# Sandwich block on one core: whole-array transposes, one bank each, and a reordered list of blocks

## The chip, the core and the metric

The kernel runs on one core of a Trainium2 chip. The metric is device time in microseconds (us); the kernel before takes 1332.34 us, the median of three runs (1331.87 to 1333.54). The engines are TensorE (PE, its weight loads apart as PEld), VectorE (DVE), ScalarE (ACT), GpSimd (POOL) and the DMA queue of SyncE (SP).

## The reference

Eight batches of 1024 rows of 256 values, all float32. Attention with 16 heads of 16 values, then a channel mix; each is added to its input after a layer norm.

```python
q = x @ w_q.T; k = x @ w_k.T; v = x @ w_v.T            # x: layer norm of the input
scores = einsum('bqhd,bkhd->bhqk', q, k) * HEAD_DIM ** -0.5
concat = softmax(scores) @ v                            # per head, then heads side by side
x = x + _layernorm(concat @ w_o.T)
xn = _layernorm(x); x_prev = xn shifted by one row
xr = mu_r * xn + (1 - mu_r) * x_prev; xk = mu_k * xn + (1 - mu_k) * x_prev
out = sigmoid(xr @ W_r.T) * (square(relu(xk @ W_k.T)) @ W_v.T)
x = x + _layernorm(out)
```

## The kernel before

**The attention loop.** A unit `u` is half a batch (512 queries); `b = u // 2`, and 16 units follow each other. A unit has 32 steps: four quads of four heads (`qd`), each over eight blocks of 128 keys (`kt`). In step `i`, PE is given `scores(i + 1)` (L579: four matmuls, two heads at a time on the two halves of the array's rows, each into its half of a two-bank tile), then one piece of other work from `pump` (L302), then `values(i)` (L601: four heads side by side, 17 columns each, into one bank that is summed over eight steps). ACT does the two exponentials of a step (L596, 128x1024 each). `scores(i + 1)` overwrites the banks that the exponentials of step `i` read, so it waits for them.

**The other work** is written as lists of words, one list for even and one for odd units (EVEN, ODD, L845); unit 0 has FIRST before it. A word is a block: `T` turns four 128-row tiles of the normalized input into `xnT` (features on partitions), `Q`, `K` and `V`/`W` are projections of the next batch from `xnT`, and `y`, `z`, `k`, `r`, `v` are the output projection, the turn and the channel mix of the unit before. `T Q K V` form the chain "ahead", `y z k r v` the chain "behind"; within a chain the order is kept, and of two chains the word that stands earlier is asked first (`choose`, L219).

**Blocks and banks.** Three banks (`PM`) serve all this work. A matmul block (class Block, cost 2) needs one bank; it goes in two halves, the input rows 0 to 63 in two steps, the rows 64 to 127 in the next two, beside the first half of the block after it. A turn (class Turn, cost 2) needs two banks: in one step eight half-array transposes (64 rows to 64 columns) go to both banks at once, in the next step the other eight with banks exchanged (`begin`, L241). When its last matmul is given out, a block's `done` gives out the copies that empty its bank; a bank may be taken again `age` (1) steps after it was freed in the program's order, and PE then waits for the copy itself. Work after a `REST` goes on one step later, two such pieces a step.

**The pace.** `pump(left)` does one piece a step, and two where the cost of the waiting words exceeds the steps that are left in the unit (L307 to L311, only after step 9 and not in two steps running):

```python
need = sum(block.cost for block in waiting) + bool(tile[0] or tile[1]) + (turning[0] is not None)
doubled[0] = not doubled[0] and need > left and step_now[0] % 32 > 9
if doubled[0] or not left: step_part(age)
```

In unit 0 `left` is 0 up to step 9, so that these steps do two pieces.

**Queries and keys.** A finished Q or K block is split in two (L378, L444), stored by SP to a scratch tensor in device memory (L448) and read back spread over heads (`spread`, L501, reads at L508, all on SP's queue in the order in which they are given out). A store waits for the reads of the same scratch half. In unit 0 only quad 0 is projected directly; quads 1 to 3 come by `spread` at the steps in FIRST_SPREADS, quads 2 and 3 with both halves of queries and keys at once (steps 9 and 10), so that they need Q10, K10, Q11 and K11 stored. The weights `wq` and `wk` are split (L881, ACT and DVE) after the first scores are given out (L941).

**After the loop** the last unit's `y z k r v` run with nothing beside them (`run_all`).

Of the kernel before, what the change touches and what calls it, by code (L numbers as in the profile page):

```python
# [56 lines left out]
def sandwich_kernel(nc, x, wpack, consts, out):  # L57
    with ExitStack() as ctx:
# [59 lines left out]
        s_first = [[sem(f"s_first{i}"), 0] for i in range(4)]  # L118
# [66 lines left out]
        turning = [None]  # L185
# [3 lines left out]
        class Block:  # L189
# [3 lines left out]
            def __init__(self, chain, half, ready, done, queued=()):  # L193
                self.chain, self.half, self.ready, self.done = chain, half, ready, done
                self.seen, self.queued = None, queued

        class Turn:

            cost, banks = 2, 2

            def __init__(self, chain, halves, ready, done):
                self.chain, self.halves, self.ready, self.done = chain, halves, ready, done
                self.seen, self.queued = None, ()
# [37 lines left out]
        def begin(age):  # L241

            took[:] = 0.0, 0.0
            block = turning[0]
            if block is None:
                block = choose(age)
                if isinstance(block, Turn):
                    turning[0] = block
                    for a in range(2):
                        tile[a] = queue(block.halves[a](PM[block.bank[a]], a), *block.waits[a])  # L250
                    ends = [None, None]
                    emit(1e9, 1e9, ends)
                    block.ends = ends
                    return False
                now[:] = block, now[0]
                if now[0] is not None:
                    tile[0] = queue(now[0].half(PM[now[0].bank[0]], 0), *now[0].waits[0])
                if now[1] is not None:
                    tile[1] = queue(now[1].half(PM[now[1].bank[0]], 1), now[1].token)
                return bool(tile[0] or tile[1])  # L260
            for a in range(2):
                tile[a] = queue(block.halves[1 - a](PM[block.bank[1 - a]], a), block.ends[1 - a])
            ends = [None, None]
            emit(1e9, 1e9, ends)
            turning[0] = None
            until_rest(block.done(block.bank, ends[1]))
            return False
# [34 lines left out]
        def pump(left, age=1):  # L302
# [4 lines left out]
            need = sum(block.cost for block in waiting) + bool(tile[0] or tile[1]) + (turning[0] is not None)  # L307
# [5 lines left out]
        def run_all():  # L313

            while waiting or tile[0] or tile[1] or now[0] or turning[0] or resting:
# [21 lines left out]
        def token_half(name, still):  # L337
# [11 lines left out]
            return half  # L349

        def turn_half(src):

            def half(m, a):
                rows = rows_of(a)
                return [(.057, lambda e, t=t: e.transpose(m[:, t * 128 + 64 * a:t * 128 + 64 * a + 64],  # L355
                                                          src(t, rows), ident[rows, rows])) for t in range(4)]
            return half
# [49 lines left out]
        def p_turn(b, g):  # L407
# [4 lines left out]
            def done(banks, p):  # L412
                cols = slice(g * 512, g * 512 + 512)
                state["xA_read"] = p

                def split(c, k, m):
                    d = copy(xnT[0][:, c, cols], m[:, :], p, state["qk_read"])
                    d = dve.op(lambda e: e.tensor_tensor(xnT[1][:, c, cols], m[:, :], xnT[0][:, c, cols].bitcast(F32),  # L418
                                                         ALU.subtract), d)
                    free_bank(k, d)  # L420
                    xnt_ready[b, c, g] = d

                split(0, banks[0], PM[banks[0]])
                yield REST
                split(1, banks[1], PM[banks[1]])
            return Turn("ahead", [turn_half(lambda t, rows, c=c: xA[rows, 4 * g + t, c * 128:c * 128 + 128])
                                  for c in range(2)], ready, done)
# [8 lines left out]
        def p_qk(b, i, mt, n):  # L436
            cols = slice(n * 512, n * 512 + 512)

            def done(k, m, p):
# [6 lines left out]
                for j in range(2):  # L446
# [6 lines left out]
                         xnt_of(b, n, "wk"), done)  # L453

        def p_v(b, g):
# [4 lines left out]
            def done(k, m, p):  # L460
# [4 lines left out]
                v_ready[b, g] = d  # L465
                state["qk_read"] = p
            return Block("ahead", token_half("wv", still), xnt_of(b, g // 2, "wv"), done)
# [3 lines left out]
        def p_direct(i, p, n):  # L471
# [23 lines left out]
            return Block("ahead", half, xnt_of(0, n, "wide"), done)  # L495
# [206 lines left out]
        def o_z(u):  # L702

            def part(c, k, m, p):
# [8 lines left out]

            def done(banks, p):
                tk["A_read"] = p
                for c in range(2):
                    part(c, banks[c], PM[banks[c]], p)
                yield from mix(u)
            return Turn("behind", [turn_half(lambda t, rows, c=c: At[rows, t, c * 128:c * 128 + 128])
                                   for c in range(2)], have(("xn2", u, 0), ("xn2", u, 1)), done)  # L720
# [85 lines left out]
        def o_v(u, g):  # L806
# [29 lines left out]
            def still(i, c, t, rows):  # L836
# [71 lines left out]
        run("T0")  # L908
# [19 lines left out]
        def sum_all():  # L928
# [7 lines left out]
                       sum_all]  # L936
        run("D00 E00 D10 E10 T1 V0 V1 E01 E11")
# [3 lines left out]
        split_weights(["wq", "wk"])  # L941
        copier[0] = "dve"

        for u in range(2 * B):
# [6 lines left out]
            for s in range(32):  # L951
# [6 lines left out]
                pump(0 if u == 0 and s < 10 else 32 - s)  # L958
# [7 lines left out]
                if u == 0:  # L966
                    for work in FIRST_SPREADS.get(s, ()):
                        spread(0, *work)
# [12 lines left out]
        for word in "y0 y1 z k0 k1 r0 r1 v0 v1".split():  # L981
# [85 lines left out]
```

How the kernel before makes its waits and increments, by code:

```python
            def on_pe(e):  # L528
                for w_ in exps + all_here + [rows_all]:
                    e.wait_ge(w_[0], w_[1])
                for u in range(16):
                    a, p, qt = u // 8, u // 4 % 2, 4 * hf + u % 4
                    rows = slice(64 * a, 64 * a + SHIFT)
                    if u >= 2:
                        e.wait_ge(g_dve, 19 * n + u - 1)
                    for kh in range(2):
                        ins = e.matmul(PS[u % 2][:, kh, :], QS[qd][rows, p, qt * 128:qt * 128 + 128],
                                       KS[qd][rows, p, kh * 512:kh * 512 + 512], start=True, stop=True)
                    ins.then_inc(g_pe, 1)
                e.wait_ge(g_dve, 19 * n + 16)
                e.transpose(PS[0][0:16, 0, 0:128], mx[:, 0:16], ident[:, :]).then_inc(g_pe, 1)
                e.wait_ge(g_dve, 19 * n + 19)
                e.wait_ge(g_sp, 128 * (n + 1))
# [4 lines left out]
            def on_dve(e):  # L548
                for u in range(16):
                    e.wait_ge(g_pe, 17 * n + u + 1)
                    if u == 0 and n:
                        e.wait_ge(g_pe, 17 * n)
                    e.tensor_reduce(mx[:, u:u + 1], PS[u % 2][:, :, :], AX.XY, ALU.max).then_inc(g_dve, 1)
                e.wait_ge(g_pe, 17 * n + 17)
                if n:
                    e.wait_ge(g_sp, 128 * n)
                e.tensor_scalar(tmp[:, 0, :], PS[0][0:16, 0, 0:128], -1.0, None, ALU.mult).then_inc(g_dve, 1)
```

## Time and profile before

| | |
|---|---|
| median of the runs | 1332.34 us |
| the profiled execution's own time | 1331.7 us |
| its span, first to last instruction | 1329.9 us |
| PE busy, matmuls | 1261.8 us (95%), 10986 instructions |
| ACT busy | 1054.8 us (79%) |
| DVE busy | 788.3 us (59%) |
| exponentials, L596 | 1024 of 1024 ns |
| transposes, L355 | 512 half-array ones, in two groups of 256 |

The profile is one execution. Busy shares are means over stages with different limits, and a matmul's busy time overlaps that of its neighbours, so the time of a step is read from one start of the scores matmuls to the next. A row of the stretches view has the stretch in us from the span's start, its length, the busy time of each engine with its instructions, PE's granted clock (1.00 is 2.4 GHz, 0.50 is 1.2 GHz), the share of time in which the 16 DMA engines were busy, and GB/s.

### The profile page before, as it was taken

The numbers are of one execution on the slowest core, as the hardware profiler recorded it, in microseconds if no ns is written. First come the engines' busy times: TensorE is split into PE (matmuls) and PEld (weight loads), VectorE is DVE, ScalarE is ACT, GpSimd is POOL, SyncE is SP. The second block draws the span as 40 slices with busy tenths as digits, with TensorE's granted clock in tenths as the row PEclk, the third lists the DMA queues.
The fourth block names the chain that finished last, engine by engine and source line by source line (L and its number), as shares of the span: only waits on it lengthen the run. The fifth ranks groups of instructions, "written<-read, shape, count | busy, mean of one in ns | idle before, by whom it ended". The sixth has DMA issues, their size and how long they took to land.

```text
span 1329.9 us, 26219 instructions
## 1 busy us (share of the span) xinstructions
PE 1261.8 (95%) x10986; PEld 649.4 (49%) x10986; DVE 788.3 (59%) x1725; ACT 1054.8 (79%) x1153; POOL 271.7 (20%) x353
## 2 busy tenths in 40 slices
PE   7879999999999999999999999999999999999944
PEld 4533455455544555455544555455554555454433
DVE  5452574857466674757577484657657474545554
ACT  2568888888878888888888888888888888888821
POOL 1000122221221222212121222113221221222120
PEclk8899999999999999999999999999999999999967
DMA  4175194115633187124833166122932166101000
GB/s 146 56 172 164 35 179 93 43 60 116 135 66 95 49 146 116 43 65 101 139 81 96 49 129 126 35 80 74 166 81 64 31 114 135 42 2 33 1 17 16
DMA packets 60776, 112.75 MB, mean 85 GB/s; under 512 B 6256, under 2 KB 31088, under 8 KB 60592
## 3 DMA queue, kind: packets, MB, share of 16 engines
q1 hardware_dynamic: 60336, 109.60, 37.0%
q8 instruction: 104, 1.70, 0.6%
q10 hardware_dynamic: 288, 1.05, 0.2%
q14 instruction: 48, 0.39, 0.1%
HBM read 68.42 MB, written 41.94 MB: 83 GB/s over the span
## 4 chain that ended last, share of the span: by engine, by line
PE 80%; DVE 11%; ACT 4%; POOL 3%; DMA 2%; issue 1%; SPq 0%; POOLq 0%; ACTq 0%
PE O L608 31%; PE S L589 22%; PE M L345 13%; PE M L332 11%; ACT PT L596 3%; DVE sth L665 2%; DVE A L674 2%; POOL rsh L670 1%; PE M L355 1%; DVE T L628 1%; DVE A L812 1%; DVE mvh L667 1%; DMA KS<-scr 1%; DVE CC L632 1%; PE M L492 1%
## 5 line engine op out<-in xcount | busy, mean ns | idle before, releaser
L596 ACT ACTIVATE PT<-S 128x1024 f32<-128x1024 f32 x1024 | 991.4, 1024 | 191.3 <-PE S L589 190.5
L608 PE MATMUL O<-PT,V 128*17 128x512 f32 x4096 | 540.8, 600 | 0.2
L589 PEld LDWEIGHTS S<-QS,KS 50*128 50x128 f32 x2048 | 185.0, 184 | 469.4 <-ACT PT L596 424.9
L589 PE MATMUL S<-QS,KS 50*128 50x512 f32 x2048 | 390.4, 452 | 13.7 <-DMA KS<-scr 6.1
L669 POOL TENSOR_SCALAR veh<-mvh 128x2 f32<-128x2 f32 x96 | 22.1, 230 | 525.2 <-DVE mvh L667 525.2
L332 PE MATMUL M<-xnT,WH 64*128 64x512 f32 x512 | 115.1, 402 | 3.3 <-DVE xnT L418 1.9
L608 PEld LDWEIGHTS O<-PT,V 128*17 128x17 f32 x4096 | 67.9, 95 | 101.6 <-issue 54.0
L812 DVE SCALAR_TENSOR_TENSOR A<-Z,M 128x512 f32<-128x512 f32 x30 | 20.4, 682 | 158.5 <-PE M L345 158.5
L345 PE MATMUL M<-WH,cT 64*128 64x256 f32 x512 | 87.5, 288 | 9.4 <-DVE cT L642 5.4
L345 PE MATMUL M<-WH,B 64*128 64x256 f32 x512 | 84.7, 281 | 3.6 <-DVE B L746 3.6
L345 PE MATMUL M<-WH,xnT 64*128 64x256 f32 x512 | 86.7, 283 | 1.4 <-DVE xnT L418 1.4
L378 DVE CAST p<-M 128x512 fp32r<-128x512 f32 x62 | 42.3, 683 | 72.2 <-PE M L332 50.9
L345 PE MATMUL M<-WH,C 64*128 64x256 f32 x512 | 83.2, 278 | 1.1 <-DVE C L776 1.1
L332 PEld LDWEIGHTS M<-xnT,WH 64*128 64x128 f32 x512 | 67.4, 189 | 14.8 <-DVE xnT L418 4.5
L345 PEld LDWEIGHTS M<-WH,cT 64*128 64x128 f32 x512 | 68.3, 193 | 12.8 <-issue 6.3
L735 POOL TENSOR_TENSOR C<-A,C 128x512 fp32r<-128x512 f32 x30 | 38.6, 1287 | 162.9 <-DVE C L378 162.9
L332 PE MATMUL M<-xnT,WL 64*128 64x512 f32 x256 | 71.5, 397 | 0.0
L332 PE MATMUL M<-C,WH 64*128 64x512 f32 x256 | 64.0, 410 | 7.6 <-DVE C L735 6.9
L670 POOL TENSOR_TENSOR rsh<-veh,half 128x2 f32<-128x2 f32 x96 | 69.0, 719 | 8.0
L345 PEld LDWEIGHTS M<-WH,xnT 64*128 64x128 f32 x512 | 67.6, 188 | 1.9 <-DVE xnT L418 1.6
L345 PEld LDWEIGHTS M<-WH,B 64*128 64x128 f32 x512 | 66.3, 187 | 4.4 <-DVE B L746 4.2
L764 POOL TENSOR_TENSOR scratch<-scratch 128x512 f32<-128x512 f32 x30 | 32.9, 1096 | 164.0 <-DVE scratch L762 164.0
(112 smaller groups left out, 1617.9 us busy)
## 6 DMA issues: line engine op xcount, KB each, us to landing
scr<-p SPq DMA_DIRECT2D x124, 256.0 KB
QS<-scr SPq DMA_DIRECT2D x60, 256.0 KB, 6.4
KS<-scr SPq DMA_DIRECT2D x60, 256.0 KB, 11.1
QS<-scr SPq DMA_DIRECT2D x66, 128.0 KB, 7.0
xA<-x_dram SPq DMA_DIRECT2D x16, 512.0 KB, 6.9
KS<-scr SPq DMA_DIRECT2D x64, 128.0 KB, 10.2
xB<-x_dram SPq DMA_DIRECT2D x16, 512.0 KB, 6.6
out_dram<-xB SPq DMA_DIRECT2D x15, 512.0 KB, 3.1
```

The costliest lines, as they stand in the source:

```text
L332: out.append((.216, lambda e, k=k, w=w, v=moving(j, c, rows): e.matmul(m[:, :], w, v, start=(a == 0 and k == 0), stop=(a == 1 and k == 5))))
L345: out.append((.117, lambda e, k=k, t=t, w=w, v=still(i, c, t, rows): e.matmul(m[:, t * 256:t * 256 + 256], v, w, start=(a == 0 and k == 0) ...
L378: return dve.op(lambda e: e.tensor_copy(dst, src), *waits)
L589: fn = lambda e, p=p, a=a, rows=rows: e.matmul(PS[p][:, a, :], KS[qd][rows, p, kt * 128:kt * 128 + 128], QS[qd][rows, p, hf * 512:hf * 512 ...
L596: e_fn = lambda e, p=p: e.activation(PT[i % 2][:, 2 * p:2 * p + 2, :], PS[p][:, :, :], ACT.Exp, scale=SCALE)
L608: fn = lambda e, j=j: e.matmul(PO[32 * j:32 * j + 17, :], V[b % 2][:, kt, 4 * qd + j, :], PT[i % 2][:, j, :], start=(kt == 0), stop=(kt == 7))
L665: toks = [dve.op(lambda e, t=t: e.bn_stats(sth[:, 2 * g + t, :], src(t)), *ready) for t in range(2)]
L670: r = pool.op(lambda e: e.tensor_tensor(rsh[:, ts], veh[:, ts], half[:, 0:2], ALU.pow), p)
L674: return dve.op(lambda e: e.tensor_scalar(dst, src, mvh[:, n, 0:1], rsh[:, n:n + 1], ALU.subtract, ALU.mult), *waits)
L735: tk["xk", u, c] = side().op(lambda e: e.tensor_tensor(C[1][:, cols], A[:, cols], C[0][:, cols].bitcast(F32), ALU.subtract), d)
L764: tk["sq", mt] = k1, r, side().op(lambda e: e.tensor_tensor(r[:, :], r[:, :], r[:, :], ALU.mult), d)
L812: d = dve.op(lambda e: e.scalar_tensor_tensor(out=A[:, cols], in0=sig_of(u, g), scalar=1.0, in1=m[:, :], op0=ALU.add, op1=ALU.mult), p, tk ...
```

## The change

A turn becomes four transposes of whole 128x128 tiles into one bank, in one step (cost 1, one bank), so each `T` and each `z` becomes two words, one for each half of the features. A turn isn't taken while the block that still has its second half to do reads the same rows of `xnT`. The lists are set anew; the key and query reads of quads 2 and 3 in unit 0 go by halves and from steps 7, 8 and 10, each with a semaphore of its own; `wq` and `wk` are split once V0 is done in the prelude; unit 0 stops doing two pieces a step one step earlier; and in steps 8 to 19 of the last two units a block is taken two steps, instead of one, after its inputs and its bank were given out. `turn_half` goes, and `p_turn`, `o_z` call `done` for one bank.

```diff
         class Turn:
-            cost, banks = 2, 2
+            cost, banks = 1, 1
...
+                    if isinstance(block, Turn) and now[0] is not None and now[0].tokens == block.tokens is not None:
+                        return None
                     waiting.remove(block)
...
+            block = choose(age)
+            if isinstance(block, Turn):
+                k, = block.bank
+                for t in range(4):
+                    fn = lambda e, t=t: e.transpose(PM[k][:, t * 128:t * 128 + 128], block.src(t), ident[:, :])
+                    if t < 3:
+                        pe.quiet(fn, *(block.waits[0] if t == 0 else ()))
+                    else:
+                        p = pe.op(fn)
+                until_rest(block.done(k, PM[k], p))
+                return False
...
-            need = sum(block.cost for block in waiting) + bool(tile[0] or tile[1]) + (turning[0] is not None)
+            need = sum(block.cost for block in waiting) + bool(tile[0] or tile[1])
...
         def p_v(b, g):
...
                 v_ready[b, g] = d
+                if meanwhile:
+                    meanwhile.pop(0)()
...
-        FIRST = "Q00 K00 V2 K01 V3 Q10 K10 Q11 K11 Q01"
-        EVEN = "W3 T0 y0 y1 T1 z k0 k1 r0 r1 v0 v1 Q00 K00 Q01 K01"
-        ODD = "y0 y1 z k0 k1 r0 r1 v0 v1 Q10 K10 Q11 K11 V0 V1 V2"
+        FIRST = "Q00 K00 V2 K01 V3 Q10 K10 K11 Q01 Q11"
+        EVEN = "W3 T00 T01 y0 y1 Q00 T10 T11 z0 z1 k0 k1 r0 r1 v0 v1 K00 Q01 K01"
+        ODD = "y0 y1 z0 z1 k0 k1 r0 r1 v0 v1 Q10 K10 Q11 K11 V0 V1 V2"
...
-        FIRST_SPREADS = {3: [(1, (0, 1), (0,), s_first[0])], 6: [(1, (1,), (1,), s_first[1])], 9: [(2,)], 10: [(3,)],
-                         16: [(0, (0,), (1,), s_first[2]), (1, (0,), (1,), s_first[3])]}
+        FIRST_SPREADS = {3: [(1, (0, 1), (0,))], 6: [(1, (1,), (1,))], 7: [(2, (0, 1), (0,))], 8: [(2, (1,), (1,))],
+                         10: [(3, (0, 1), (0,)), (3, (1,), (1,))], 16: [(qd, (0,), (1,)) for qd in range(4)]}
...
-        run("T0")
+        run("T00 T01")
...
         meanwhile[:] = [lambda: ln1_norm(0, 1), lambda: (split_weights(["wv"]), sum_heads()),
-                       sum_all]
-        run("D00 E00 D10 E10 T1 V0 V1 E01 E11")
+                       sum_all, lambda: None, lambda: split_weights(["wq", "wk"])]
+        run("D00 E00 D10 E10 T10 T11 V0 V1 E01 E11")
...
         scores(0)
-        split_weights(["wq", "wk"])
...
-                pump(0 if u == 0 and s < 10 else 32 - s)
+                age = 2 if b + 1 == B and 8 <= s < 20 else 1
+                pump(0 if u == 0 and s < 9 else 32 - s, age)
...
-        for word in "y0 y1 z k0 k1 r0 r1 v0 v1".split():
+        for word in "y0 y1 z0 z1 k0 k1 r0 r1 v0 v1".split():
```

## Rows read from the trace of the kernel before

**Rows 1.** The page: its first line, and the line of busy times.

```profile
span 1329.9 us, 26219 instructions
...
PE 1261.8 (95%) x10986; PEld 649.4 (49%) x10986; DVE 788.3 (59%) x1725; ACT 1054.8 (79%) x1153; POOL 271.7 (20%) x353
```

**Rows 2.** Stretches view, units 0, 2, 3, 14 and 15, from scores to scores.

```profile
41.42:135.28 93.86, 84.53 (x609) 38.69 (x609) 40.28 (x81) 64.67 (x70) 3.81 (x5) 0.91 0.56 140
...
210.38:287.45 77.07, 75.83 (x676) 37.55 (x672) 47.57 (x98) 64.69 (x71) 16.05 (x20) 1.00 0.32 76
287.45:362.37 74.92, 74.84 (x692) 39.63 (x688) 49.37 (x116) 64.74 (x71) 18.61 (x24) 1.00 0.53 107
1122.61:1197.12 74.51, 72.38 (x608) 34.92 (x604) 39.60 (x89) 64.40 (x71) 18.23 (x23) 1.00 0.17 37
1197.12:1268.75 71.63, 69.73 (x568) 31.51 (x564) 37.10 (x84) 62.34 (x69) 16.17 (x22) 1.00 0.05 16
```

**Rows 3.** Stretches view, PE alone: steps 1, 2-3, 4, 10-12 of unit 2; 29-30 of unit 0.

```profile
212.73:215.12 2.39, 2.39 (x28) 1.00 0.99 156
215.12:219.31 4.19, 4.05 (x44) 1.00 1.04 137
219.31:222.60 3.29, 2.63 (x28) 1.00 0.94 194
234.44:243.18 8.74, 8.33 (x70) 1.00 0.00 1
129.22:133.17 3.95, 3.75 (x28) 1.00 0.47 140
```

**Rows 4.** Timeline of PE, unit 2, steps 2 to 4: start, length, line.

```profile
215.12 0.74 PE L589 MATMUL S<-QS,KS 50*128 50x512 f32 x4
215.68 0.42 PE L355 MATMUL M<-ident,xA 64*128 64x64 f32 x8
216.03 1.05 PE L608 MATMUL O<-PT,V 128*17 128x512 f32 x8
217.02 1.13 PE L589 MATMUL S<-QS,KS 50*128 50x512 f32 x4
...
220.72 0.35 PE L345 MATMUL M<-WH,cT 64*128 64x256 f32 x1 [0.66 <-POOL xB L823]
```

**Rows 5.** Groups by line, whole-array 128x128 products of the prelude: count, busy us, mean ns.

```profile
L897 PE MATMUL S<-A 128*128 128x128 f32 x16 | 2.1, 281 | 1.6 <-DMA A<-w_dram 1.6
L897 PEld LDWEIGHTS S<-A 128*128 128x128 f32 x16 | 1.9, 191 | 2.4 <-DMA A<-w_dram 2.4
```

**Rows 6.** Timeline of DVE, unit 2: the second splits after turns.

```profile
219.88 0.69 DVE L418 TENSOR_TENSOR xnT<-M,xnT 128x512 fp32r<-128x512 f32 x1
...
237.19 0.69 DVE L418 TENSOR_TENSOR xnT<-M,xnT 128x512 fp32r<-128x512 f32 x1
```

**Rows 7.** Stretches view, PE alone: unit 0, steps 0-1, 2-9 and 14-16.

```profile
41.42:53.71 12.29, 10.53 (x42) 0.58 0.00 1
53.71:78.14 24.43, 24.43 (x221) 1.00 0.51 151
87.84:102.28 14.44, 8.35 (x59) 0.76 1.04 159
```

**Rows 8.** Timeline of PE, unit 0: the waits in step 0 and at step 15.

```profile
44.18 1.22 PE L332 MATMUL M<-xnT,WH 64*128 64x512 f32 x2 [1.35 <-DVE WL L881]
...
95.89 1.22 PE L589 MATMUL S<-QS,KS 50*128 50x512 f32 x4 [6.09 <-DMA KS<-scr]
```

**Rows 9.** DMA view, 50 to 135 us, key reads: count, KB each, median us to landing.

```profile
KS<-scr SPq DMA_DIRECT2D x8, 128.0 KB, 4.6
...
KS<-scr SPq DMA_DIRECT2D x4, 256.0 KB, 10.7
```

**Rows 10.** Stretches view, PE alone: unit 14, step 18.

```profile
1163.07:1166.53 3.46, 2.81 (x19) 1.00 0.02 5
```

**Rows 11.** Timeline of PE after the loop: the first block waits.

```profile
1274.11 0.55 PE L345 MATMUL M<-WH,cT 64*128 64x256 f32 x1 [5.36 <-DVE cT L642]
```

More of the change, by code:

```diff
@@ L117, in sandwich_kernel @@
         s_qk = [[sem(f"s_qk{i}"), 0] for i in range(4)]
-        s_first = [[sem(f"s_first{i}"), 0] for i in range(4)]
+        s_first = [[sem(f"s_first{i}"), 0] for i in range(10)]
         s_rows, s_wide = [sem("s_rows"), 0], [sem("s_wide"), 0]
@@ L191, in sandwich_kernel, with __init__ @@
             cost, banks = 2, 1
-            def __init__(self, chain, half, ready, done, queued=()):
+            def __init__(self, chain, half, ready, done, queued=(), tokens=None):
                 self.chain, self.half, self.ready, self.done = chain, half, ready, done
-                self.seen, self.queued = None, queued
+                self.seen, self.queued, self.tokens = None, queued, tokens
         class Turn:
-            cost, banks = 2, 2
-            def __init__(self, chain, halves, ready, done):
-                self.chain, self.halves, self.ready, self.done = chain, halves, ready, done
-                self.seen, self.queued = None, ()
+            cost, banks = 1, 1
+            def __init__(self, chain, src, ready, done, tokens=None):
+                self.chain, self.src, self.ready, self.done = chain, src, ready, done
+                self.seen, self.queued, self.tokens = None, (), tokens
         def until_rest(work):
@@ L243, in begin @@
             took[:] = 0.0, 0.0
[L244 to L267, printed above, removed]
+            block = choose(age)
[9 more added lines that the diff above has]
+                return False
+            now[:] = block, now[0]
+            if now[0] is not None:
+                tile[0] = queue(now[0].half(PM[now[0].bank[0]], 0), *now[0].waits[0])
+            if now[1] is not None:
+                tile[1] = queue(now[1].half(PM[now[1].bank[0]], 1), now[1].token)
+            return bool(tile[0] or tile[1])
         def emit(limit0, limit1, ends):
@@ L313, in run_all @@
         def run_all():
-            while waiting or tile[0] or tile[1] or now[0] or turning[0] or resting:
+            while waiting or tile[0] or tile[1] or now[0] or resting:
                 pump(0, 0)
@@ L348, in half @@
                 return out
[L349 to L356, printed above, removed]
             return half
@@ L405, in ln1_norm, with p_turn, done @@
             state["ln1"][b, g] = d
-        def p_turn(b, g):
+        def p_turn(b, g, c):
             def ready():
                 return (state["ln1"][b, g], c_here) if (b, g) in state["ln1"] else None
-            def done(banks, p):
+            def done(k, m, p):
                 cols = slice(g * 512, g * 512 + 512)
                 state["xA_read"] = p
[L416 to L427, printed above, removed]
+                d = copy(xnT[0][:, c, cols], m[:, :], p, state["qk_read"])
+                d = dve.op(lambda e: e.tensor_tensor(xnT[1][:, c, cols], m[:, :], xnT[0][:, c, cols].bitcast(F32),
+                                                     ALU.subtract), d)
+                free_bank(k, d)
+                xnt_ready[b, c, g] = d
+            return Turn("ahead", lambda t: xA[:, 4 * g + t, c * 128:c * 128 + 128], ready, done, g)
         def xnt_of(b, g, *more):
@@ L465, in done @@
                 v_ready[b, g] = d
+                if meanwhile:
+                    meanwhile.pop(0)()
                 state["qk_read"] = p
-            return Block("ahead", token_half("wv", still), xnt_of(b, g // 2, "wv"), done)
+            return Block("ahead", token_half("wv", still), xnt_of(b, g // 2, "wv"), done, tokens=g // 2)
         def p_direct(i, p, n):
@@ L494, in half @@
                 return out
-            return Block("ahead", half, xnt_of(0, n, "wide"), done)
+            return Block("ahead", half, xnt_of(0, n, "wide"), done, tokens=n)
         meanwhile = []
@@ L700, in o_y, with o_z, done @@
             return Block("behind", token_half("wo", still), have(("cT", u, 0), ("cT", u, 1), more=("wr",)), done)
[L702 to L704 removed]
+        def o_z(u, c):
+            def done(k, m, p):
                 d = copy(Z[:, c, 1:513], m[:, :], p, tk.get("Z_read"), *(part_read[2] if u == 0 else ()))
@@ L712, in part @@
                 tk["z", c] = [d, d0]
[L714 to L720, printed above, removed]
+                if c:
+                    tk["A_read"] = p
+                    yield from mix(u)
+            return Turn("behind", lambda t: At[:, t, c * 128:c * 128 + 128], have(("xn2", u, 0), ("xn2", u, 1)), done)
         def mix(u):
@@ L967, in sandwich_kernel @@
                     for work in FIRST_SPREADS.get(s, ()):
-                        spread(0, *work)
+                        spread(0, *work, s_first.pop())
                 if u == 0 and s in (2, 3, 4, 5):
```

3 lines of the change are left out of this document (1 added, 2 removed).

## The prediction

> **What bounds the kernel.** I read the page first. PE is busy for 95% of the span, ACT for 79% [rows 1]. That is a mean, so I cut the loop into units with the stretches view, from the start of one step's scores to another's. There the reader sees three kinds of unit: unit 0 takes 93.86 us, even units such as unit 2 take 77.07, odd units such as unit 3 take 74.92 [rows 2] (units 4, 6, 8, 10 and 12 repeat the one, 1 to 13 the other). Then single steps. A step with half a block in it takes about 2.36 us, scores, half block and values end to end on PE: (74.92 - 4.19) / 30 if the two transposing steps of an odd unit cost what those of unit 2 cost [rows 2, 3]. The step of 2.39 in [rows 3] is one of these. A step with nothing in it takes 3.95 / 2 = 1.98 [rows 3]: there ACT's exponentials set the pace. So PE sets a step that has work, ACT one that has none, and a unit's time is the sum over its steps plus what PE waits for. 32 steps at 2.36 make 75.5; unit 0 and the even units lie above what their work needs.
>
> **Where the even unit loses.** Steps 2 and 3 hold the two phases of T0 and take 4.19. Step 4 takes 3.29: PE starts its half block 1.41 after the scores (219.31 to 220.72) where 0.56 is usual (215.12 to 215.68) [rows 3, 4]. The row names POOL's add, but y0 doesn't read that; the bank it takes is one that T0 gave back, and DVE's split of it ends at 219.88 + 0.69 = 220.57 [rows 6]. Steps 10 to 12 take 8.74 [rows 3]: T1 waits two steps for a second bank, both its phases fall in a doubled step 10, Q00 then waits for `xnT`, and step 12 is doubled, since the words still waiting cost more than the steps left. z takes steps 14 and 15, 4.2 as in T0. Together 4.19 + 3.29 + 8.74 + 4.2 = 20.42 for eight steps.
>
> **A turn's price, step by step.** Before, eight half-array transposes stand between scores and values for 0.35 (215.68 to 216.03); scores take 0.56 before them, values 0.99 to the next scores (216.03 to 217.02) [rows 4]. Afterwards four 128x128 transposes stand there. The trace has no such transpose; the nearest row is the prelude's whole-array float32 product, 16 records in 2.1 us with a mean of 0.281, so (2.1 - 0.28) / 15 = 0.12 from start to start, its weight loads of 0.191 hidden beside them [rows 5]. I take 4 x 0.12 + 0.1 to drain = 0.58, and a step of 0.56 + 0.58 + 0.99 = 2.13, against 4.19 / 2 = 2.10 before. From below, 0.35 as before, and ACT's 1.98 is the floor. From above, 0.24 a transpose, since the eight products of L897 show as 16 records and a transpose might need two as well: 1.06, a step of 2.61. I take 0.12 because today's transposes show one record each (512 for 512). So a turn is no faster on PE: what may be gained is that it needs one bank and no second phase.
>
> The Trainium skill, in "TensorE: Matmul & The Clock Gate", section "Part 4: PE-mode transpose", speaks against this price: about 275 ns for one 128x128 transpose inside a kernel. If that were the spacing, the four would take 4 x 0.275 + 0.1 = 1.2 and the step 2.75, and the sum below would come out as about 1342. Today's eight in 0.42 us [rows 4] don't bear that out as a spacing.
>
> **The even unit after.** I walked the new list through the rule for choosing. Steps 0-1 W3; 2 T00; 3 T01; 4-5 y0; 6-7 y1; 8-9 Q00; 10 T10; 11 T11; 12-13 K00; 14 z0; 15 z1; 16-19 Q01, K01; 20-31 k, r, v. The need never exceeds the steps left (22 of 22 at step 10, 20 of 20 at step 12), so nothing is doubled, and step 8, where the second half of y1 had gone alone, carries Q00. T00's split is given to DVE one step earlier, ahead of v1's norm, so the bank that y0 takes is free in time: the 0.85 wait goes. Next late is DVE at step 11. It is full in that stretch, T11 takes the bank that T10 has just left, and the matching split ended at 237.19 + 0.69 = 237.88, 3.44 after step 10's scores at 234.44 [rows 3, 6]; T11 wants it at 2.13 + 0.56 = 2.69, so it waits 0.75 and the values behind it on PE, and then ACT, wait along. Sum of the same eight steps: T00, T01, T10, z0, z1 5 x 2.13, T11 2.13 + 0.75, y0 and K00 2 x 2.36 = 18.25. Saved: 2.2 a unit, six units (2 to 12): **-13**. Odd units keep their order; two turns at +0.03: **+0.4** over seven.
>
> **Unit 0.** Step 0: PE waits 1.35 for the split of `wk` [rows 8], and the copies for it stand between ACT's exponentials. Steps 0 and 1 take 12.29 at a mean clock of 0.58 [rows 7], that is mostly at 1.2 GHz, after a stretch in which PE had little to do. With the weights split in the prelude, beside V1, the wait and the two ACT copies (about 1.2) go: 1.5 off for certain. If PE, busy sooner, keeps 2.4 GHz, the two steps take about 3.7 + 3.05 = 6.75, that is 5.5 off. The rows don't tell which; I take **-3.5** and keep both ends. Steps 2 to 9 hold two pieces and take 24.43 / 8 = 3.05 [rows 7]; step 9 now has one: -0.7, and step 10 carries half a block in place of a doubled turn: **-1** together. The large term is the wait for keys: steps 14 to 16 take 14.44, 6.09 of it a wait for the key read of quad 2, and PE comes back at half clock (0.76 on average) [rows 7, 8]. Before, the whole read was given out in step 9 (at 78.14 - 3.05 = 75.1) and the keys landed 20.8 later. Now the first halves go out in step 7, without Q11 and K11 before them (one 3.05 step less), and as half reads, 4.6 to land (a group that mixes quad 1's half reads with parts of whole ones) and not 10.7 [rows 9]: about 20.8 - 3.05 - 6.1 = 11.7 after step 7 begins. They are wanted at step 15, 2 x 3.05 + 6 x 2.3 = 19.9 after it. A margin of 8, so the wait goes and steps 13 to 16 (16.8) become two half blocks and two turns, 9.4 with 0.4 for DVE: **-7.4**. What could be late next on SP's queue, the second half of these keys (a store that waits for the first read, then 4.6) and quad 3's, is wanted four and eight steps later. The 16 reads at step 16 hold up batch 1's stores, and DVE may stand for some 10 us on a store, as it does today; nothing on PE needs it before unit 1. The last half block ends one step earlier: **-0.4**. Prelude: the copy of a turn's first half need not wait for its second phase, T00/T01 and T10/T11: **-1** (0 to -1.5).
>
> **The last two units.** With age 2, z starts a step later and k0 two steps later in unit 14; the wait in step 18 (3.46 against 2.36 [rows 10]) and that before z go, -2.5. But two steps of v1 move into unit 15, its y0 waits 0.9 longer for `cT`, and its own v1 ends after the loop. There y0 stands 5.36 behind the last quad's DVE work [rows 11], and now about four more DVE operations of 0.7 [rows 6] come before it: up to +2.8, I take +2.2. With z0's copy starting earlier at the end: **0** together (-2.5 to +3).
>
> **Sum** against the profiled execution's 1331.7 (span 1329.9): -13 + 0.4 - 3.5 - 1 - 7.4 - 0.4 - 1 + 0 = -25.9, so 1305.8. That run stands 0.6 below the median of 1332.34; I say **1306**. Its own range: -2 to +2 for the clock of steps 0-1, -9 if a turn is only as long as ACT's step (58 turns in the loop x 0.15), +5 for a turn dearer by 0.08, 3 each way for the last units: 1296 to 1314.
>
> **Rivals.** (1) *The first unit keeps its wait.* The scratch goes through one SP queue with stores that wait for reads, and DMA engines are full there (share 1.04) [rows 7]; if the first halves come no sooner and PE falls to 1.2 GHz again, -7.4 and 2 of the 3.5 are lost: 1315. Against it: less than half as much is read at once. Chance 0.16. (2) *The even units slip a step.* The plan fits exactly, so one late bank means a doubled step, and T11's wait takes the place of y0's; at worst 77.07 stays: 1319. Chance 0.1. (3) *Whole-array transposes don't hide their weight loads.* Each then shows its load and its matmul, 0.191 + 0.12 [rows 5]: 4 x 0.31 + 0.1 = 1.34, 0.76 more in each of 58 turn steps, all on PE: +44, **1350**, slower. It decides from 25.9 / 58 = 0.45 a turn on, or 0.23 from one transpose to the next; two records each (0.24) would give about 1334. For it: today two row halves load beside each other, which ends. Against it: [rows 5] hide the load on the whole array. Chance 0.07.
>
> **Chances.** Forecast 0.67, rivals 0.16, 0.1 and 0.07. Leaving out (3) and the edges, 1296 to 1320 holds 8 in 10. A measurement of this kernel can tell 0.2%, 2.7 us. Faster 0.92, same 0.02, slower 0.06.
>
> **What would show it.** In the profile after: 8 x 16 x 2 = 256 transposes of 128x128; turn steps near 2.13 with a start-to-start of 0.12; no wait before y0; about 0.75 of waiting in step 11 behind DVE's split; even units near 74.9; no DMA wait of PE in unit 0, which takes about 81.5, and clock 1.00 from its step 2 on; y0 after the loop later by about 2. I am wrong if transposes are 0.2 or more apart, if even units stay above 76, or if PE still waits for `KS<-scr`.

## The result and the profile after

The changed kernel takes 1315.38 us, the median of four runs (1312.64 to 1317.79), beside 1332.11 (1331.22 to 1333.54) for the kernel before on the same chip: a ratio of 0.9873, 95% interval 0.9851 to 0.9894. It is faster by 1.3%. The forecast of 1306 was 9 us too low. The wide range (1296 to 1320) holds the result; the forecast's own (1296 to 1314) misses it by 1.4, and the number lies on the 1315 of rival 1, so it takes the profile to say which mechanism it was. The profiled execution took 1315.18, so it can be set against the one before: 16.5 us less.

First the page, span and busy times, to be read against [rows 1]:

```profile
span 1313.4 us, 25725 instructions
...
PE 1260.9 (96%) x10730; PEld 645.5 (49%) x10730; DVE 783.2 (60%) x1726; ACT 1056.3 (80%) x1153; POOL 271.0 (21%) x352
```

256 matmul records fewer (512 half-array transposes became 256), yet PE's busy time is the same. So nearly all of the gain is time in which PE had stood still. The stretches view, units 0, 2, 3 and 14 from scores to scores, and unit 15 to the end of the last exponential (columns as in [rows 2], whose last row ends 1.1 later, with the last values):

```profile
39.47:122.43 82.96, 81.95 (x593) 37.70 (x594) 37.72 (x77) 63.41 (x68) 3.82 (x5) 0.96 0.53 145
...
198.07:273.55 75.48, 75.03 (x652) 36.82 (x648) 46.67 (x98) 64.82 (x71) 16.10 (x20) 1.00 0.31 78
273.55:348.84 75.29, 75.29 (x685) 39.80 (x682) 49.39 (x116) 64.82 (x71) 18.65 (x24) 1.00 0.52 106
1102.51:1175.14 72.63, 71.49 (x588) 33.58 (x584) 37.34 (x82) 64.32 (x71) 16.03 (x20) 1.00 0.18 38
1175.14:1248.40 73.26, 70.73 (x553) 32.13 (x550) 35.84 (x81) 62.39 (x69) 15.82 (x20) 0.98 0.05 16
```

Against [rows 2], unit 0 gives 10.9, an even unit 1.6, an odd one loses 0.2 to 0.5. Of the end, the fairest row is one stretch from the start of unit 14 to the last instruction. After it took 210.89 us; before, with the numbers of [rows 2] and [rows 1], 1329.9 - 1122.61 = 207.29. So the last two units lose 3.6. Added up: start of the loop 41.42 to 39.47, -1.95; unit 0 -10.9; unit 1 +0.5; six even units -9.5; six odd ones +1.7; the end +3.6. That is the whole of the 16.5.

The stretches view again, PE alone, to be read against [rows 3, 7]: two turn steps, a step of half a block, T10 to K00's first step, and of unit 0 the steps 0-1, 2-8 and 13-16 (columns: stretch, length, PE busy, granted clock, DMA share, GB/s).

```profile
202.81:205.03 2.22, 2.22 (x21) 1.00 1.12 135
205.03:207.34 2.31, 2.31 (x22) 1.00 1.01 169
207.34:209.69 2.35, 2.35 (x29) 1.00 0.36 82
221.53:228.93 7.40, 6.95 (x54) 1.00 0.00 1
39.47:49.32 9.85, 9.44 (x42) 0.65 0.01 2
49.32:70.72 21.40, 21.40 (x196) 1.00 0.48 147
79.94:89.31 9.37, 9.37 (x65) 1.00 0.35 102
```

y0's step is back at 2.35 from 3.29, and steps 13 to 16 of unit 0 take 9.37 without a wait for DMA, where three of them took 14.44. A pair of turn steps takes 4.53, where the two phases took 4.19. The timeline of PE shows why, steps 2, 3 and 11 of unit 2 (start, length, line), to be read against [rows 4]:

```profile
202.81 0.72 PE L572 MATMUL S<-QS,KS 50*128 50x512 f32 x4
203.46 0.66 PE L251 MATMUL M<-ident,xA 128*128 128x128 f32 x4
204.04 1.05 PE L591 MATMUL O<-PT,V 128*17 128x512 f32 x8
205.03 0.81 PE L572 MATMUL S<-QS,KS 50*128 50x512 f32 x4
205.77 0.66 PE L251 MATMUL M<-ident,xA 128*128 128x128 f32 x4
206.35 1.05 PE L591 MATMUL O<-PT,V 128*17 128x512 f32 x8
...
223.76 0.79 PE L572 MATMUL S<-QS,KS 50*128 50x512 f32 x4
225.01 0.66 PE L251 MATMUL M<-ident,xA 128*128 128x128 f32 x4 [0.46 <-DVE xnT L404]
```

The four transposes hold values up for 0.58 (203.46 to 204.04, 205.77 to 206.35), as forecast to the hundredth. But they begin 0.65 and 0.74 after the scores, where the half-array transposes of a turn's first phase began after 0.56. Those of its second phase began after 0.97, which the prediction passed over; their scores lasted 1.13 [rows 4]:

```profile
217.99 0.41 PE L355 MATMUL M<-ident,xA 64*128 64x64 f32 x8
```

Why T01's begin some 0.08 later than T00's can be read from ACT's timeline of the changed kernel:

```profile
200.97 1.94 ACT L579 ACTIVATE PT<-S 128x1024 f32<-128x1024 f32 x2 [0.33 <-PE S L572]
203.34 1.94 ACT L579 ACTIVATE PT<-S 128x1024 f32<-128x1024 f32 x2 [0.44 <-PE S L572]
```

The exponentials whose banks the scores take end 0.10 after T00's scores begin (202.91), and 0.25 after T01's (205.28), because T00's step is shorter than the usual 2.36. T01's scores last 0.81 and not 0.72, and its transposes follow later by as much.

In the last two rows of PE's timeline T11 begins 1.25 after its scores, behind DVE's split of T10's bank.

### The profile page after: what moved, and what is told of

Same layout as the page of the kernel before. It is cut to its first block, busy times and chain, and to the rows that moved or that the text cites. A ratio compares the mean times of both kernels' runs of the same rounds, so it can differ in the third digit from the quotient of the medians.

```text
span 1313.4 us, 25725 instructions
## 1 busy us (share of the span) xinstructions
PE 1260.9 (96%) x10730; PEld 645.5 (49%) x10730; DVE 783.2 (60%) x1726; ACT 1056.3 (80%) x1153; POOL 271.0 (21%) x352
## 3 DMA queue, kind: packets, MB, share of 16 engines
q10 hardware_dynamic: 288, 1.05, 0.2%
## 4 chain that ended last, share of the span: by engine, by line
PE 88%; DVE 6%; ACT 3%; POOL 1%; issue 1%; DMA 0%; POOLq 0%; ACTq 0%
PE O L591 35%; PE S L572 24%; PE M L341 14%; PE M L328 11%; PE M L251 3%; ACT PT L579 2%; DVE sth L648 1%; DVE A L657 1%; POOL rsh L653 1%; PE M L475 1%; DMA A<-w_dram 0%; DVE mvh L650 0%; DVE xB L672 0%; DVE xnT L404 0%; DVE T L611 0%
## 5 line engine op out<-in xcount | busy, mean ns | idle before, releaser
L572 PE MATMUL S<-QS,KS 50*128 50x512 f32 x2048 | 385.7, 451 | 6.1 <-ACT PT L579 6.1
L328 PE MATMUL M<-xnT,WH 64*128 64x512 f32 x512 | 111.9, 397 | 0.0
L741 DVE TENSOR_SCALAR scratch<-M 128x512 f32<-128x512 f32 x32 | 22.1, 692 | 77.9 <-PE M L328 69.1
```

Source lines behind the costliest of these rows:

```text
L328: out.append((.216, lambda e, k=k, w=w, v=moving(j, c, rows): e.matmul(m[:, :], w, v, start=(a == 0 and k == 0), stop=(a == 1 and k == 5))))
L572: fn = lambda e, p=p, a=a, rows=rows: e.matmul(PS[p][:, a, :], KS[qd][rows, p, kt * 128:kt * 128 + 128], QS[qd][rows, p, hf * 512:hf * 512 ...
L741: d = dve.op(lambda e: e.tensor_scalar(r[:, :], m[:, :], 0.0, None, ALU.max), p, *f1)
```

## Experiments

Each kernel is the changed one with one edit, if not said otherwise; all times are medians, and the ratio is to the kernel before on the same chip. Three chips served, on which the kernel before has medians of 1331.59 to 1333.93, so a microsecond or two between medians of different kernels tells nothing.

**The looser pace.** The first two kernels take it away, in both last units or in the last alone.

```diff
-                age = 2 if b + 1 == B and 8 <= s < 20 else 1
+                age = 1
```

> The looser pace taken away, all else as in the changed kernel (1315.4 us; unit 14 72.6, unit 15 73.2, 65.0 after the loop's last exponential). Theory (the pace moves v1's last pieces past the end of the unit, where they stand on DVE ahead of the cT that y0 waits for, and this costs more than the waits it saves): unit 14 back to about 74.6, unit 15 to about 70.7, the end to 62.3, together 3 less, so about 1312. Rival A (the two last units lost their time to the turns, not to the pace): units 14 and 15 stay at 146 together and the time at 1315. Rival B (the pace pays): 1318.

```diff
-                age = 2 if b + 1 == B and 8 <= s < 20 else 1
+                age = 2 if u == 2 * B - 2 and 8 <= s < 20 else 1
```

> The looser pace in unit 14 alone. Theory: unit 14 keeps its 72.6, unit 15 still has v1's chain on DVE ahead of cT in its first steps (step 3 near 4.8), but v1 of unit 15 ends within the loop and the end falls from 65.0 to about 62.3: about 1313.5. Rival (what comes after the loop is longer because of the turns there): the end stays at 65 and the time at 1315 or above.

Without it: 1312.61 us (1311.86 to 1313.63), ratio 0.9849 (0.9826 to 0.9872). In unit 14 alone: 1313.74 (1311.19 to 1314.76), ratio 0.986. The runs of the two overlap each other's and the changed kernel's (1312.64 to 1317.79), so medians alone don't rank the three. The profiles say more. First the one without the looser pace, unit 14 and unit 15, PE alone:

```profile
1102.85:1177.83 74.98, 72.78 (x601) 1.00 0.17 36
1177.83:1248.72 70.89, 68.97 (x552) 1.00 0.05 16
```

Then the one that has it in unit 14 alone, the same two stretches:

```profile
1102.13:1174.67 72.54, 71.40 (x590) 1.00 0.18 38
1174.67:1247.05 72.38, 70.03 (x564) 1.00 0.05 16
```

From unit 14 to the last instruction the two take 208.15 (1102.85 to the span of 1311.0) and 207.27 (1102.13 to 1309.4), the changed kernel 210.89. In unit 14 the looser pace saves 2.4 (74.98 to 72.54), as priced (2.5); unit 15 pays 1.5 back for the part of v1 that moves into it. In unit 15 it moves v1 behind the loop: from the end of the last exponential to the last instruction the changed kernel takes 65.0 (1313.4 - 1248.4), these two 62.3 (1311.0 - 1248.72) and 62.35. The kernel before takes 62.26, since its last exponentials end at 1265.70 + 1.94 = 1267.64 (ACT's timeline):

```profile
1265.70 1.94 ACT L596 ACTIVATE PT<-S 128x1024 f32<-128x1024 f32 x2 [0.41 <-PE S L589]
```

PE's timeline of the changed kernel, the first block after the loop, to be read against [rows 11]:

```profile
1257.71 0.55 PE L341 MATMUL M<-WH,cT 64*128 64x256 f32 x1 [6.60 <-DVE cT L625]
```

How v1 stands in the way in unit 15 shows in step 3 of the changed kernel, PE's timeline:

```profile
1182.41 0.49 PE L572 MATMUL S<-QS,KS 50*128 50x512 f32 x2 [0.39 <-ACT PT L579]
1183.59 0.39 PE L341 MATMUL M<-WH,cT 64*128 64x256 f32 x1 [0.68 <-POOL cT L625]
...
1184.50 1.91 PE L591 MATMUL O<-PT,V 128*17 128x512 f32 x8
1186.34 1.22 PE L572 MATMUL S<-QS,KS 50*128 50x512 f32 x4
```

and DVE's, the same stretch:

```profile
1179.45 0.68 DVE L791 SCALAR_TENSOR_TENSOR A<-Z,M 128x512 f32<-128x512 f32 x1
1180.16 0.75 DVE L648 BATCH_NORM_STATS2 sth<-A 128x6 f32<-128x256 f32 x2
...
1181.04 0.68 DVE L622 STREAM_TRANSPOSE T<-CC 128x512 f32<-128x512 f32 x1
1181.76 0.43 DVE L366 CAST cT<-T 128x512 fp32r<-128x512 f32 x1
```

v1's gating and statistics now stand on DVE ahead of the transpose that makes `cT`, and y0 waits for it on PE. Behind that wait values take 1.91, where they take 1.05 elsewhere: the clock has fallen. The stretches view has step 3 of the changed kernel,

```profile
1181.53:1186.34 4.81, 3.74 (x23) 0.80 0.01 2
```

and of the kernel with K00 ahead (below), whose last units have the same list and pace:

```profile
1178.67:1182.58 3.91, 2.88 (x22) 1.00 0.00 0
```

The step after it takes 3.03 in the one and 2.35 in the other. So 0.9 + 0.68 = 1.6 of the 3.6 lost is a clock that fell in one profile and not in the other; the other 2 is the looser pace in unit 15, which the kernel without it there doesn't lose (207.27, beside 207.29 before). That kernel has the same wait in step 3 too, at a clock of 1.00 and in 3.94, not near the 4.8 expected. Six kernels here have the pace in both units: in the profiles of three the clock fell at this place (0.98, 0.95 and 0.95 in unit 15), in three it did not; in the five without the pace in unit 15 it never did. Why it falls in one and not in the next stays open.

**The price of a transpose.** Each of the four is done twice, into the same place.

```diff
                 for t in range(4):
                     fn = ...
+                    pe.quiet(fn, *(block.waits[0] if t == 0 else ()))
                     if t < 3:
-                        pe.quiet(fn, *(block.waits[0] if t == 0 else ()))
+                        pe.quiet(fn)
                     else:
                         p = pe.op(fn)
```

> Each transpose of a turn is given out twice into the same place, so a turn has eight and the output is unchanged. 58 turns lie in the loop. Theory (0.12 us from one transpose to the next, all on PE's path): 4 x 0.12 = 0.5 more in each turn's step, 2.27 becoming 2.75, 58 x 0.5 = 28 more, about 1343. Rival A (a transpose costs 0.24, as two records): 0.96 a step, 56 more, 1371. Rival B (a turn's step is set by ACT or by the change of the array's shape and not by the transposes): under 10 more, below 1325.

1340.49 us (1337.98 to 1341.31), ratio 1.0052 (1.0029 to 1.0074). PE's timeline, step 3 of unit 2 of this kernel:

```profile
208.34 0.73 PE L573 MATMUL S<-QS,KS 50*128 50x512 f32 x4
209.00 1.09 PE L251 MATMUL M<-ident,xA 128*128 128x128 f32 x8
210.03 1.05 PE L592 MATMUL O<-PT,V 128*17 128x512 f32 x8
```

Four more transposes cost 1.09 - 0.66 = 0.43, that is 0.11 each; 58 turns make 24.9, and the medians differ by 25.1 (1340.49 - 1315.38). That they agree so well is in part luck. T11's step doesn't grow (2.82): there the transposes wait for DVE anyway. And T01's grows only from 2.31 to 2.67, since here it begins 0.66 after its scores, as T00 does: behind the longer T00 step the exponentials are done in time.

**The entry to the whole array.** The same bank and the same single step, but half-array transposes, the upper half after the lower.

```diff
-                for t in range(4):
-                    fn = lambda e, t=t: e.transpose(PM[k][:, t * 128:t * 128 + 128], block.src(t), ident[:, :])
+                p = None
+                for a, t in itertools.product(range(2), range(4)):
+                    rows = slice(64 * a, 64 * a + 64)
+                    fn = lambda e, t=t, rows=rows: e.transpose(
+                        PM[k][:, t * 128 + rows.start:t * 128 + rows.stop], block.src(t)[rows, :], ident[rows, rows])
+                    waits = () if t else (p,) if a else block.waits[0]
```

> The changed kernel's words and banks, but each turn made of eight half-array transposes into one bank: four of rows 0 to 63, then, after these have ended, four of rows 64 to 127 (the halves can't write one bank at once). This tells the plan (one bank, one step) from the whole array. Theory (the gain of the even units is the plan's; the whole array only makes the single step short enough): eight in turn at 0.06 and one wait of about 0.3 make 0.85 and not 0.58 between scores and values, the turn's step 2.45, 58 turns, 10 more: 1325. Rival A (whole arrays carry the gain): even units back near 77, the time 1330 or more. Rival B (the form doesn't matter): 1315.

1325.84 us (1323.49 to 1326.1), ratio 0.9933 (0.991 to 0.9955). PE's timeline, step 3 of unit 2:

```profile
207.43 0.72 PE L576 MATMUL S<-QS,KS 50*128 50x512 f32 x4
207.99 0.92 PE L253 MATMUL M<-ident,xA 64*128 64x64 f32 x8
208.84 1.05 PE L595 MATMUL O<-PT,V 128*17 128x512 f32 x8
```

These begin 0.56 after the scores, as in the first phase before the change, and the doubled whole-array transposes above began after 0.66 in the same step. So 0.1 of the later start belongs to the whole-array form behind half-array scores, and the further 0.08 of T01 to ACT's exponentials. But one half after the other takes 0.85 in place of 0.58, and the step is 2.40: of these two ways to use one bank, the whole array is the cheaper. What in the array causes the 0.1, no run here shows. Unit 2 takes 76.31 in this kernel, between 77.07 and 75.48: about half of the even units' gain is the plan's, the other half needs the whole array.

**The first unit's order.** The old list, the old reads and the old pace in unit 0, the rest of the change kept.

```diff
-        FIRST = "Q00 K00 V2 K01 V3 Q10 K10 K11 Q01 Q11"
+        FIRST = "Q00 K00 V2 K01 V3 Q10 K10 Q11 K11 Q01"
...
-        FIRST_SPREADS = {3: [(1, (0, 1), (0,))], 6: [(1, (1,), (1,))], 7: [(2, (0, 1), (0,))], 8: [(2, (1,), (1,))],
-                         10: [(3, (0, 1), (0,)), (3, (1,), (1,))], 16: [(qd, (0,), (1,)) for qd in range(4)]}
+        FIRST_SPREADS = {3: [(1, (0, 1), (0,), s_first[0])], 6: [(1, (1,), (1,), s_first[1])], 9: [(2,)], 10: [(3,)],
+                         16: [(0, (0,), (1,), s_first[2]), (1, (0,), (1,), s_first[3])]}
...
-                pump(0 if u == 0 and s < 9 else 32 - s, age)
+                pump(0 if u == 0 and s < 10 else 32 - s, age)
```

> The first unit's list, reads and pace as before the change, the rest as changed (early weights and turns too). Theory (the reads by halves and two steps earlier take the wait for keys away): PE waits for the key read again at step 15, 5 to 7 us, steps 13 to 16 take about 16.8 and not 9.4, unit 0 about 91 and not 83, so 8 more: 1323.5. Rival (the wait had gone with the turns and the earlier start, the reads matter little): unit 0 stays below 85 and the time near 1316.

1326.61 us (1322.77 to 1328.51), ratio 0.995 (0.9931 to 0.9968): 11.2 of the 16.7 are gone. In its profile unit 0 takes 93.39, 10.4 more than in the changed kernel. PE's timeline shows the wait of [rows 8] again, and values at half speed behind it:

```profile
94.30 1.22 PE L572 MATMUL S<-QS,KS 50*128 50x512 f32 x4 [7.00 <-DMA KS<-scr]
...
96.72 1.91 PE L591 MATMUL O<-PT,V 128*17 128x512 f32 x8
```

Which of the three (list, reads, pace) takes the wait away was not run apart.

**The split of the query and key weights.** Put back behind the first scores.

```diff
         meanwhile[:] = [lambda: ln1_norm(0, 1), lambda: (split_weights(["wv"]), sum_heads()),
-                       sum_all, lambda: None, lambda: split_weights(["wq", "wk"])]
+                       sum_all]
...
         scores(0)
+        split_weights(["wq", "wk"])
```

> wq and wk are split after the first scores again, as before the change; the rest as changed. Theory (the split held up Q00 and put two copies between ACT's exponentials): the wait of about 1.3 for the split of wk in step 0 is back, steps 0 and 1 take about 12.3 and not 9.9, PE still falls to half clock there; start of step 0 unchanged within 0.5: 2.4 more, about 1317.8. Rival (these steps are long because of the clock alone): steps 0 and 1 stay below 10.5 and the time within 1 of 1315.4.

1315.48 us (1313.78 to 1318.96), ratio 0.9863 (0.9837 to 0.989): no different from the changed kernel, against what I expected. PE's timeline and the stretch of steps 0-1 in its profile:

```profile
40.44 1.22 PE L328 MATMUL M<-xnT,WH 64*128 64x512 f32 x2 [1.05 <-DVE WL L861]
```

```profile
37.68:49.20 11.52, 10.35 (x42) 0.58 0.01 2
```

The wait is back and the two steps take 11.52 in place of 9.85. But they begin at 37.68, and end at 49.20 where the changed kernel ends them at 49.32. Of the kernels here, eight have the changed kernel's prelude (its own profile among them): they begin the loop between 38.93 and 41.35, and seven of them (the eighth keeps PE busy there, the last kernel below) end step 1 of unit 0 between 48.64 and 51.21. So moving the split shifts time from the loop into the prelude and is worth nothing that can be told. What makes the start differ by 2 us among kernels with the same prelude stays open: PE's mean clock from 20 us to the first steps doesn't order them (0.91 and 0.82 both go with 38.93, 0.84 with 41.35).

**K00 ahead of T10.** In the even units' list, so that T11 finds DVE done.

```diff
-        EVEN = "W3 T00 T01 y0 y1 Q00 T10 T11 z0 z1 k0 k1 r0 r1 v0 v1 K00 Q01 K01"
+        EVEN = "W3 T00 T01 y0 y1 Q00 K00 T10 T11 z0 z1 k0 k1 r0 r1 v0 v1 Q01 K01"
```

> In EVEN the word K00 stands before T10 and T11 and not behind z1, all else as changed. In the changed kernel T11 (step 11 of an even unit) takes the bank that T10 has just left and waits for DVE's split. Theory (DVE is full there because of the two norms of y, and the wait is DVE's): T10 and T11 fall into steps 12 and 13, T11 gets a bank that was left earlier, its step is 2.3 and not 2.82, even units 75.0 and not 75.5, six of them, 3 less: 1312.3. Rival (the wait moves along: DVE is late in step 13 too, or K00 waits in step 10): even units stay at 75.5 and the time at 1315.

1311.06 us (1310.93 to 1311.26), ratio 0.9822 (0.98 to 0.984), and its interval lies below that of the changed kernel. The stretches view of PE, steps 10-12 and step 13 of unit 2, where T11 is now:

```profile
222.12:229.05 6.93, 6.93 (x56) 1.00 0.00 1
229.05:231.36 2.31, 2.31 (x21) 1.00 0.49 113
```

PE waits for nothing there any more; even units take 74.9, which makes 3.4 over six. Of the other 0.9 in the profiles (4.3 by the spans), the last two units give 1.4, where the clock did not fall this time, and unit 0 takes back 0.7.

**All at once.** Both edits (no looser pace, K00 ahead) with Q11 of unit 0 set behind T01 and the load of `xB` released by the last split of a weight instead of the first.

```diff
-                for word in FIRST.split():
+                for word in FIRST.split()[:-1]:
                     block(0, -1, word)
             for word in (EVEN, ODD)[hf].split():
                 block(b + 1, u - 1, word)
+                if u == 0 and word == "T01":
+                    block(0, -1, FIRST.split()[-1])
...
-                s_xb[hf], out_done[hf], split_of["wr"])
+                s_xb[hf], out_done[hf], split_of["wvf"])
```

> Three edits to the changed kernel together: no looser pace, K00 before T10, and in unit 0 the word Q11 behind T01, so that Q00 of the next batch finds its xnT given out in time and Q11's second half doesn't go alone for two steps (the first load of xB waits for the last weight split, for safety). Theory (the three are independent): -3 for the pace, -3 for T11's wait, two steps of unit 0 at 1.98 in place of 2.36, -0.7: about 1308.7. Rival (Q11 later holds up SP's reads of queries for unit 1): unit 1 starts with a wait and 1311 or more is left.

1321.45 us (1320.51 to 1325.14), ratio 0.9908: a miss of 12.7. One step of unit 0 takes 13.8. PE's timeline:

```profile
102.29 1.12 PE L251 MATMUL M<-ident,xA 128*128 128x128 f32 x4 [10.13 <-DVE p L425]
```

and DVE's:

```profile
100.82 0.69 DVE L366 CAST p<-M 128x512 fp32r<-128x512 f32 x1 [15.81 <-DMA scr<-p]
```

DVE stands 15.81 us before the cast that reuses a projection's buffer, because the store out of that buffer is given out behind sixteen reads and `xB` on SP's queue (at 94.06); the split that T11 wants stands behind the cast. In the changed kernel DVE stands on such a store too, but later, when PE has nothing that needs DVE before unit 1:

```profile
118.19 0.69 DVE L366 CAST p<-M 128x512 fp32r<-128x512 f32 x1 [9.60 <-DMA scr<-p]
```

Where Q11 stands thus seems to decide whether that stand costs 10 us or nothing. It was moved together with the load of `xB`, and the two were not run apart; the other two edits are not it, since alone they take 83.59 for unit 0 (next kernel), and all four 94.63.

**The two edits without unit 0's, and PE kept busy at the start.** The second of these kernels adds two matmuls without use behind the first scores.

> The looser pace left out and K00 set before T10 in the list of the even units, the rest as in the changed kernel. Theory: both costs stand in different units (the last two, and the even ones), so the two gains add: 2.8 + 4.3 us below the changed kernel's 1315.4, 1308.3 us (1307 to 1310); T11's step 2.30, even units 74.9, units 14 and 15 together 145.9, the last exp to the end 62.3. Rival: the gain of the looser pace's absence was only that PE's clock did not happen to fall in unit 15; then 1311, as with K00 alone.

```diff
         scores(0)
+        for i in range(2):
+            tk["On_read"] = pe.op(lambda e: e.matmul(PO[:, :], On[:, 0:128], On[:, :], start=True, stop=True),
+                                  on_set, tk["acc_free"])
```

> As the kernel with both edits, and two matmuls of 128x512 without use, into the bank that values has not yet begun, between the first scores and the second ones, where PE stood idle for 1.88 us behind ScalarE's first exp. Theory: PE falls to 1.2 GHz in steps 0 and 1 because it was idle there; filled, it keeps 2.4 GHz, and the 6.8 to 10.2 us that the profiles have at 1.2 GHz there lose a third to a half: steps 0 and 1 together about 7 instead of 9.9 to 10.9 us, 1305.0 us (1304 to 1306.5). Rival 1: the clock falls anyway (what went before in the prelude sets it) and the two matmuls cost up to 1 us: 1308 to 1309. Rival 2: steps 0 and 1 are bound by the exp and not by PE: no gain, 1308.

The two edits: 1310.15 us (1309.16 to 1311.52), ratio 0.9817 (0.9776 to 0.9859); above what the sum of the gains had given, and no better than K00 alone by more than the runs scatter. The rival (the pace cost nothing but the clock, 1311) is not ruled out by the medians; in the profiles the end takes 1307.4 - 1099.12 = 208.3 and 1309.1 - 1099.67 = 209.4 with K00 alone, both with a clock of 1.00 in the last units, so about 1 us is the pace's own. With the two matmuls: 1307.36 (1305.64 to 1310.72), ratio 0.98 (0.9756 to 0.9844), the best of all. The gap that they fill, in PE's timeline of the kernel without them:

```profile
38.97 0.50 PE L572 MATMUL S<-QS,KS 50*128 50x512 f32 x2 [1.88 <-ACT PT L579]
```

The stretches view, steps 0-1 of unit 0, PE alone, without and with them:

```profile
38.97:48.67 9.70, 9.29 (x42) 0.65 0.01 3
```

```profile
38.93:45.69 6.76, 6.35 (x43) 1.00 0.00 1
```

That is 2.9 us in the profiles and 2.8 in the medians, though the runs of the two kernels overlap. In its profile the granted clock is 1.00 from the loop's start to its end, so the clock behind that idle time, and not the exponentials, made these steps long.

## Why the prediction was right, and where it was off

The direction and most of the places came out as forecast; the size did not (-16.5 in place of -25.9), and some mechanisms did not. By its own steps:

- **Unit 0, the keys: right.** -7.4 was forecast for steps 13 to 16; they went from 16.78 to 9.37, and the old order, reads and pace put back cost 10.4 in this unit, the clock included. Rival 1 (the wait stays) is out, though the time is the one it gave. That the four steps sum to the 9.4 of the working is luck: it had two half blocks, two turns and 0.4 for DVE there, but the turns fell in steps 11, 12, 17 and 18, and these are four steps with one half block each. Steps 9 and 10 gave their -1. The -0.4 at the end of the unit did not come: of Q11 and Q00 one half each goes alone, and the last half block goes in step 26, one step later than before, not one earlier.
- **Steps 0-1 and the prelude: right in sum, wrong in its terms.** -3.5 and -1 were forecast, -2.4 and -1.95 came. But the -3.5 was put down to the split of the weights, and taking that back changed nothing: step 1 then ends at 49.20, as against 49.32, and 53.71 before the change. Which part of the changed prelude gives these 4.4, no run here separates. The lower end of the estimate, 6.75 for the two steps at full clock, is what the last kernel shows (6.76); the split was not what stood in its way, the idle time before it was.
- **The even unit: the step that failed is "scores take 0.56 before them".** It was carried over from half-array transposes. Whole-array ones begin 0.65 to 0.74 after the scores (0.1 for the form, 0.08 for ACT in the second turn of a pair), so a turn step is 2.22 to 2.31 and not 2.13. The 0.58 behind it is right as a sum, with 0.11 for a transpose and not 0.12. Five of them and T11's make the eight steps about 0.6 longer than the 18.25 of the working: -1.6 a unit, not -2.2. The rest held: y0's wait is gone, no step is doubled, the steps come in the order that was walked, and T11 waits behind DVE's split (0.5 to 0.6; forecast 0.75). So rival 2 (a slipped step) is out. That this wait could be had for a word moved was not seen.
- **Odd units:** the same later start in both turns makes +0.3 where +0.06 was counted (+0.03 a turn).
- **The last two units: the other term that failed.** 0 was forecast between -2.5 and +3, +3.6 came. Unit 14 gave 1.9 of the 2.5. From the end of the last exponential the kernel takes 2.7 more (62.26 to 65.0), where 2.2 was taken. Unit 15 to that point takes 2.7 more too (1267.64 - 1197.12 = 70.52 to 73.26): its wait was priced at 0.9, and in this profile the fallen clock cost 1.6 on top.
- **Rival 3 and the spacing: settled.** In the groups by operation the 128 transposes of `T` read

```profile
L251 PE MATMUL M<-ident,xA x128: 272/273/477, 11.4 to 979.1; 128*128 128x128 f32 x128
```

with a median of 273 ns each, and (0.66 - 0.27) / 3 = 0.13 from one start to the next. So rival 3 (0.31 apart, 1350) is out: a load stays hidden. The 275 ns of the Trainium skill ("TensorE: Matmul & The Clock Gate", "Part 4: PE-mode transpose") (its case is bf16, here it is float32) agree with the length of one record, and are not the spacing here.

The forecast's error of 9.4 is made up of 3.5 in the even units, 1.8 in the odd ones, 3.6 at the end and 1.4 in unit 0, less 1 in the prelude. The largest part is the price of the start of a turn (the even and odd units); of the 3.6 at the end about 1.6 is the clock behind a short wait, as this profile has it.

## What to carry to other kernels

When a group of instructions on PE is replaced by one of another shape, price the seam to the neighbours too, not only the group's own spacing: here the four transposes cost what they should, and 0.1 more stood in front of them in each of 58 turns, or 0.18 where a turn followed a turn, because a shorter step leaves less time to the engine whose work it waits for. When a resource is reused one step later than it was freed (one bank, T10 then T11), the wait sits on the engine that empties it; look for a block that needs neither and set it between, which was worth 3.4 us in the even units (six by 75.48 - 74.92) for one word moved. And a looser pace moves work into the next unit, where its operations stand ahead of what that unit needs first: price both units.

## What the runs showed of the hardware

- PE's clock can fall behind short waits, in one profile and not in the next: in unit 15 of the changed kernel it fell to 1.2 GHz in a step with 0.39 and 0.68 us of waiting, in two other kernels with the same waits in that step (0.38 and 0.65, 0.39 and 0.67) it stayed at 2.4 GHz. At the start of the loop PE stood idle for 1.88 us behind the first exponential, and steps 0-1 ran at a mean clock of 0.65; with two matmuls without use in that gap it was 1.00, and the two steps took 6.76 in place of 9.70 (one profile of each).
- Whole-array transposes behind half-array scores began 0.1 us later than half-array transposes did there (0.66 beside 0.56); from one to the next it is 0.11 to 0.13 us, with records of 0.27.
- A store given out late on SP's queue held DVE, which wanted the store's source buffer, for 15.81 us, and through it PE for 10.13, which had nothing to do with the transfer.
